# Projections of a fused block: the keys and values turned as 32-row tiles in one stretch per chunk, their sums a chunk late, the queries' relu moved from GpSimd to VectorE

## What is computed

```python
qkv = jnp.einsum('bchw,oc->bohw', gn(x), w_qkv)              # 768 channels from 256
y = depthwise 5x5 conv of qkv, then a grouped 1x1 conv
q = relu(mqkv[:, :, :DIM]); k = relu(mqkv[:, :, DIM:2 * DIM]) # mqkv: qkv and y, by heads
v = jnp.pad(mqkv[:, :, 2 * DIM:], one row of ones)
vk = jnp.einsum('bhdn,bhen->bhde', v, k)                      # sums over all points
out = jnp.einsum('bhde,bhen->bhdn', vk, q)
out = out[:, :, :-1] / (out[:, :, -1:] + ATT_EPS)             # then w_proj and a scale and shift
x = x + out
```

## Time and profile before

| | |
|---|---|
| median of 3 runs | 2473.91 us (2470.03 to 2474.42) |
| the profiled execution, its span | 2473.8 us |
| PE busy | 2359.6 us, 95% |
| VectorE busy | 1994.9 us, 81% |
| ScalarE busy | 1495.6 us, 60% |
| GpSimd busy | 1099.8 us, 44% |
| the page's slices 5 to 17, the projections | PE 9 (99 for most), DVE 7 or 8, ACT 5 or 6, POOL 7 or 8 tenths |
| products of the projections (L1132), 2304 matmuls | 319.2 + 303.5 + 301.9 us |
| GpSimd's relu of the queries (L939), 126 instructions | 239.1 us |

### The profile page before, as it was taken

The page is one execution under the profiler, slowest core; times in us unless marked ns, Lnnn a source line. Parts: engine busy times, 40 slices in busy tenths (PEclk is TensorE's granted clock), DMA queues, the critical chain, the costliest instruction groups (busy, mean ns, idle before and its releaser), DMA issues. The chain is left out here.

```text
span 2473.8 us, 66794 instructions
## 1 busy us (share of the span) xinstructions
PE 2359.6 (95%) x25485; PEld 1881.3 (76%) x25485; DVE 1994.9 (81%) x2653; ACT 1495.6 (60%) x1864; POOL 1099.8 (44%) x1476
## 2 busy tenths in 40 slices
PE   5999799999999999799999999999999889999998
PEld 5889688877777887577888888888888656666666
DVE  7887688878788877778888888888888588888775
ACT  5777566666566666566776776677767434433442
POOL 7722387887787878200000000000000068888887
PEclk9999899999999999899999999999999999999999
DMA  7874689988988989988888888888888777777774
GB/s 285 336 301 173 208 295 344 329 293 314 316 288 323 344 299 302 253 196 207 209 209 208 209 210 207 210 208 209 207 208 210 228 243 280 275 275 271 271 272 136
DMA packets 300973, 628.38 MB, mean 254 GB/s; under 512 B 50784, under 2 KB 252256, under 8 KB 291552
## 3 DMA queue, kind: packets, MB, share of 16 engines
q1 hardware_dynamic: 295072, 590.38, 77.5%
q10 hardware_dynamic: 4688, 31.63, 3.6%
q0 software_dynamic: 1008, 3.67, 0.4%
HBM read 327.81 MB, written 300.94 MB: 254 GB/s over the span
## 5 line engine op out<-in xcount | busy, mean ns | idle before, releaser
L1562 PE MATMUL c_ps<-dh,wh 128*128 128x512 f32 x1152 | 465.3, 404 | 15.8 <-DVE wl L1712 9.9
L1477 ACT ACTIVATE dh<-image 128x1632 fp32r<-128x1632 f32 x192 | 301.5, 1570 | 269.9 <-PE c_ps L1562 254.8
L1562 PE MATMUL c_ps<-dh,wl 128*128 128x512 f32 x1152 | 456.4, 396 | 0.0
L1562 PE MATMUL c_ps<-dl,wh 128*128 128x512 f32 x1152 | 454.6, 395 | 1.6 <-issue 1.6
L1921 POOL TENSOR_TENSOR ql<-image,qh 128x1024 fp32r<-128x1024 f32 x1 | 2.4, 2359 | 967.8 <-DVE ql L2152 967.8
L1670 DVE TENSOR_TENSOR dl<-image,dh 128x1632 fp32r<-128x1632 f32 x192 | 356.3, 1856 | 73.9 <-ACT dh L1477 73.9
L1132 PE MATMUL o_ps<-xh,wqh 128*128 128x512 f32 x768 | 319.2, 416 | 11.3 <-issue 8.4
L1909 POOL TENSOR_TENSOR ql<-image,qh 128x1024 fp32r<-128x1024 f32 x126 | 300.9, 2413 | 10.7 <-ACT qh L1940 10.7
L1132 PE MATMUL o_ps<-xl,wqh 128*128 128x512 f32 x768 | 303.5, 395 | 0.0
L1132 PE MATMUL o_ps<-xh,wql 128*128 128x512 f32 x768 | 301.9, 393 | 0.0
L1562 PEld LDWEIGHTS c_ps<-dh,wh 128*128 128x128 f32 x1152 | 218.5, 190 | 68.6 <-DVE wl L1712 10.0
(11 more groups left out here) (212 smaller groups left out, 5107.8 us busy)
## 6 DMA issues: line engine op xcount, KB each, us to landing
qkv_scratch<-stage SPq DMA_DIRECT2D x384, 408.0 KB, 4.7
image<-qkv_scratch SPq DMA_DIRECT2D x189, 816.0 KB, 6.3
yq_scratch<-qy SPq DMA_DIRECT2D x64, 512.0 KB, 6.7
image<-qr_scratch SPq DMA_DIRECT2D x128, 256.0 KB, 6.1
image<-yq_scratch SPq DMA_DIRECT2D x128, 256.0 KB, 5.3
ox<-x_scratch SPq DMA_DIRECT2D x8, 4096.0 KB, 15.3
qr_scratch<-qs SPq DMA_DIRECT2D x126, 256.0 KB, 3.6
out<-ox SPq DMA_DIRECT2D x7, 4096.0 KB, 12.7
```

The source lines that it names most:

```text
L1477: act.activation(dh[kind][:, :], raw[kind], ACT.Copy).then_inc(hi_ready, 1)
L1562: last = pe.matmul(c_ps[:, m, :], w[hp][:, kind, part, o:o + P], cells[:, :, HALF * dy:HALF * dy + HALF * NB], start=(k == 0), stop=(k == 5))
```

## The change

In `projections`:

- The turns become 64 transposes of 32 rows by 128 columns (`turn(n)`), all in one stretch after product 5, into four banks (`t_ps` has one for each 32 rows; keys in the left half, values in the right). ScalarE reads them in two instructions of 128x1024, `take_k` and `take_v`, at the start of the next chunk.
- The sums of chunk n - 1 stand after product 5 of chunk n, in front of the turns; those of the last chunk come after the loop.
- The waits for the sums and turns (`small_ready`) are set in front of the last matmul of product 5. They have a new one: in chunk 5 it waits for `var`, since `stat_ps` is now the first four columns of a turned bank; in chunk 1 for the reading of the sums. The matmul of the means waits for ScalarE's readings of the chunk before.
- VectorE reads the sums in chunk 1 of the next image, after the queries' differences. The mean is copied out of PSUM first. `variance()` stands before the copy of product 5.
- The queries' relu `qs` goes from GpSimd (two instructions of 128x512) to VectorE (one of 128x1024), behind the queries' differences.
- `pause` goes. GpSimd's `edge` is now a tensor_tensor with a column of zeros as one operand. The border's memset stands between edge and copy.

In `output`, the table `K["vk"]` has B + 1 places, and its two halves are read by instructions of their own.

```diff
@@ projections, GpSimd
-                        pause(1 + u, n)
+                        if u == 0 and n % 4 < 2:
+                            queries_free(pool, b, n)
                         edge(kv, 2 * u, 2 * u, n)
+                        if u == 0 and n % 4 < 2:
+                            border(n)
                         pool.tensor_copy(staged(2 * u, n, 2), every_second(kv, 2 * u, n, 1 - n % 2)).then_inc(kv_odd, 1)
...
                         if n % 2:
-                            pool.tensor_scalar(staged(j0, n, 0, 0, 1), every_second(buf, t0, n, 0, 1), -1.0, None, ALU.mult)
+                            pool.tensor_tensor(staged(j0, n, 0, 0, 1), none, every_second(buf, t0, n, 0, 1), ALU.subtract)
                         else:
-                            pool.tensor_copy(staged(j0, n, 1, HALF - 1, HALF), every_second(buf, t0, n, NB - 1, 1))
+                            pool.tensor_tensor(staged(j0, n, 1, HALF - 1, HALF), every_second(buf, t0, n, NB - 1, 1), none, ALU.add)
...
-                        for t in range(2):
-                            last = pool.tensor_scalar(qs[:, n % 2, t, :], qw[:, n % 2, t, :], 0.0, None, ALU.max)
-                        last.then_inc(qs_ready, 1)
@@ projections, ScalarE
+            def take_k(g):
+                act.wait_ge(t_full, 2 * g + 2)
+                at_least(act, vk_full, g)
+                act.activation(kT[:, :, :, :].rearrange("p u a (r c) -> p r (u a) c", r=NSQ),
+                               kt_ps.rearrange("p r (a c) -> p r a c", c=SQ), ACT.Relu).then_inc(k_turned, 1)
...
+                        if before:
+                            take_k(g - 1)
                         key(0)
+                        if before:
+                            take_v(g - 1)
@@ projections, TensorE
                     for w, xx in ((wh, xh), (wl, xh), (wh, xl)):
+                        if k == 5 and ahead is not None:
+                            ahead()
...
+            def small_ready(b, n):
+
+                g = NCH * b + n
+                at_least(pe, k_turned, g)
+                at_least(pe, v_turned, g)
+                if n == 1:
+                    at_least(pe, vk_taken, 2 * b)
+                if n == 5 and not (isinstance(b, int) and b == B - 1):
+                    pe.wait_ge(ns["var"], b + 2)
...
+                pe.wait_ge(kv_ready, 2 * g + 2)
+                pe.wait_ge(kv_ready_v, 2 * g + 2)
+
+            def turn(n):
+
+                for s, out in ((0, kt_ps), (1, vt_ps)):
+                    for u in range(2):
+                        for a in range(4):
+                            for r in range(NSQ):
+                                rows = slice(SQ * r, SQ * r + SQ)
+                                last = pe.transpose(out[:, r, SQ * (4 * u + a):SQ * (4 * u + a) + SQ],
+                                                    kv[rows, n % 2, 2 * u + s, P * a:P * a + P], K["ident"][rows, rows])
+                    last.then_inc(t_full, 1)
...
                         product(b, n, 2)
-                        turn(b, n, 0)
...
                         product(b, n, 3)
-                        product(b, n, 4)
                         if variances:
                             variances()
-                        turn(b, n, 1)
-                        product(b, n, 5)
-                        for u in range(2):
-                            sum_vk(b, n, u)
+                        product(b, n, 4)
+                        product(b, n, 5, lambda: small_ready(b, n))
+                        if not (isinstance(b, int) and b == 0 and n == 0):
+                            sum_vk((n - 1) % NCH)
+                        turn(n)
@@ projections, VectorE
+                        at_least(dve, K["qr_stored"][n % 2], 32 * (4 * b + n // 2))
+                        dve.tensor_scalar(qs[:, n % 2, :, :], qw[:, n % 2, :, :], 0.0, None, ALU.max).then_inc(qs_ready, 1)
...
                         if n > 0:
                             queries(n - 1)
+                        if n == 1 and not (isinstance(b, int) and b == 0):
+                            sums_out(b - 1, bass.ds(B if isinstance(b, int) and b == 1 else b - 1, 1))
...
+                        if nxt and n == 5:
+                            variance()
                         dve.wait_ge(o_full, QT * g + 6)
@@ output, VectorE
-                for c in range(2):
-                    last = dve.tensor_tensor(ks[par][:, :, c, HT * c:HT * c + HT], heads.unsqueeze(1).broadcast_to([P, KT, HT]),
-                                             at[:, :, 0, D:D + 1].broadcast_to([P, KT, HT]), ALU.mult)
+                for t, at in halves:
+                    for c in range(2):
+                        last = dve.tensor_tensor(ks[par][:, t:t + 2, c, HT * c:HT * c + HT], heads.unsqueeze(1).broadcast_to([P, 2, HT]),
+                                                 at[:, :, 0, D:D + 1].broadcast_to([P, 2, HT]), ALU.mult)
```

## The result

| | before | after |
|---|---|---|
| median, 4 runs each | 2474.16 us | **2616.57 us** (2614.77 to 2619.55) |
| ratio, 95% interval | | **1.0576** [1.0563, 1.0589] |
| span of the profiled execution | 2473.8 us | 2617.8 us |
| TensorE's start in the next stage | 1005.3 us | 1151.3 us (+146.0) |

The rest of the program is 2 us shorter, so all of the loss lies in the projections. The direction was forecast, the size was not: +57 against +142.

The account below looks back on a forecast made before the run. TensorE bounds the projections; after the change VectorE's chain, with 0.5 us slack, would set most chunks. Ordinary 19.5, chunk 1 8.2, chunk 0 -4.8, chunk 5 30.8 + 0.5, ends and output 3: +57, 2531 us, range 2464 to 2564.

Parts of the forecast that it names:

- What bounds the kernel: Projections: TensorE is the bound, busy 88.6 of 89 us an image; VectorE's real slack is 0.5 us a chunk.
- TensorE's part: Each chunk: two stretches of turns out, one of 64 small turns in, -0.6 us; TensorE would allow a 10.3 us period.
- Ordinary chunks: 39 chunks (2, 3, 4, 6, 7 of eight images, without the last): VectorE sets the period, +0.5 us each, +19.5.
- GpSimd's reads: VectorE's chain: GpSimd's SBUF reads hold two-input instructions; 1.2 us a chunk in place of 0.97, so +0.23.
- Rival B: VectorE's chain: relu and `xl` both held by a GpSimd copy, 1.65 us a chunk; 2548 us in all, chance 0.18.
- The clock: Chunk 5 only: after some 4 us idle TensorE's granted clock falls to 0.50, adding 1.1 us.
- The stream: The 64 turns take 1.12 us as in the convolution stage; their going one after another was given nothing.
- Chunk 1: Eight chunks at +0.5 us, plus 0.6 in seven for reading the sums before the second value copy: +8.2.
- Chunk 5: Seven images: TensorE's last matmul of product 5 waits for `var` behind `xl`, +4.4 us each, +30.8.
- The signs: Expected after: TensorE waiting 0.5 to 1 us for `xl`, busy below 85 of 90, turns 1.1, chain 8.1 or more.
- Rival A: GpSimd's reads fall under copies from PSUM, the 0.97 us of collisions goes to zero: 2462 us, chance 0.15.
- The port pair: By the skill's whole-instruction lock, GpSimd's reads would cost VectorE 3.4 us a chunk, over 100 in all.

Follow-up runs that it names:

- e: Kernel before with the queries' relu on VectorE, waiting additions out and two-input edges; turns, sums and statistics as before: 2524.41 us, 1.0206.
- q: g with the turns as 16 transposes of 128x128 in place of 64 of 32 rows: 2464.97 us, 0.9955.
- m: h with the turns as 16 transposes of 128x128 in place of 64 of 32 rows: 2463.75 us, 0.9952.
- r: m with the turns as 32 transposes of 64 rows in place of 16 of 128x128: 2446.69 us, 0.9889.
- h: g with product 0 starting with its four matmuls of `xh` and waiting for `xl` only behind them: 2495.52 us, 1.0102.
- f: Kernel after with three more matmuls of 128x512, never read, behind each chunk's turns: 2592.66 us, 1.0471.
- g: c with `variance()` moved up behind the second value copy of chunk 5: 2497.05 us, 1.0093.
- d: Kernel after with `variance()` moved up in chunk 5, in front of the differences of keys and values 1: 2576.97 us, 1.0409.
- c: Kernel after with the relu on GpSimd again and GpSimd's waiting additions and one-input edges back: 2519.82 us, 1.0174.
- b: Kernel after with GpSimd's waiting additions and one-input edges back; the relu stays on VectorE: 2544.82 us, 1.0276.
- s: e with 48 never-read matmuls of the sums' form (96 instructions) between each chunk's sums of u = 0 and 1: 2691.80 us, 1.0878.
- o: e with 48 small never-read transposes added behind each chunk's sums: 2780.61 us, 1.1239.

## Why the prediction was wrong in size, step by step

**What bounds the kernel, TensorE's part.** Right. The slack of VectorE was as read: e, which lengthens its chain alone, is 51 us slower. q, m and r show the other side of it: with VectorE's chain left alone and few enough instructions, TensorE's savings come through. The turns take 1.1 us, a chunk of h 10.2 (forecast 10.3).

**Ordinary chunks: the step that failed.** Forecast +19.5 for the 39 of them, measured +88.9 (443.3 to 532.3 us). Of these e, with the same work on VectorE and the clock full, has 39.8, twice the forecast; the other 49 are slow clock, for the most part, and stalls, which the sum put at nothing in these chunks. Three terms:
- GpSimd's reads. I had counted 1.65 us a chunk and then took 1.2, because the relu, with one input, was "mostly not" held. It is: 1.07 against 0.72. The row that I relied on the earlier trace rows was of an instruction half as long in another stage. The full count gives 3.03 + 7.21 + 0.65 + 0.68 + 0.14 = 11.71, and the trace shows 11.8. Rival B's mechanism held, not its 2548, which leaves out clock and stalls as well (and by its own 0.45 for each of the 54 chunks would have been 2555). The relu's own 0.75 was right (0.72).
- The clock. I charged it only behind the 4 us idle of chunk 5. It also falls behind two idles of 0.5 and 0.8 us with the sums and turns between them, and costs about 1.5 us in each of 28 of the 39 chunks, some 42 us. No row of before had shown a fall without a long idle, and I took that for a condition; f shows that filling the idle brings the clock back in about half of these chunks.
- The stream. Forecast nothing ("the rows of the convolution stage are the same instruction"). The time of an instruction was right, but not that so many could be had. The stage from which I took the row has as many small ones beside 54 long matmuls in 14.5 us, 12.5 instructions a us; a chunk of 10.2 us with 36 long ones asks for 16. The stalls in the turns and at the loop's turn are 25 us in the stage, where before it was 4.5, and each is followed by slow matmuls; q to g puts 32 us on the 64 turns as such.

**Chunk 1**: +8.2 forecast, +18.5 measured, three of the eight with a stall. **Chunk 0**: -4.8 and -0.9. **Chunk 5**: +30.8 forecast for seven, **+34.7 measured**; after to d and c to g give 40 and 23 for the wait. That the sum came so near is in part luck, as its pieces did not. The order was as read, `var` directly behind `xl` and the products behind it; in image 6:

```profile
1008.40 1.65 DVE L1248 TENSOR_TENSOR xl<-xn,xh 128x1024 fp32r<-128x1024 f32 x1
1009.97 0.15 DVE L134 TENSOR_SCALAR p_ve<-pt_ps 128x2 f32<-128x2 f32 x1
```

```profile
1010.33 0.47 PE L1133 MATMUL o_ps<-xl,wqh 128*128 128x512 f32 x1 [2.59 <-issue]
1010.74 0.77 PE L1168 MATMUL psum_ps<-vT,kT 128*32 128x33 f32 x64
1011.43 1.87 PE L1159 MATMUL pt_ps<-ident,kv 32*128 32x32 f32 x64
```

TensorE starts 0.2 us after `var`, and the turns then take 1.87 us at the lower clock. But the idle is 2.4 to 2.6 us in place of 4. I had VectorE work on end from one `xl` to the next, 12.9 us; here it takes 14.6 (995.45 to 1010.05), because it waits 2 us for product 1, in front of which stand an idle of TensorE of 0.96 us without a semaphore and seven matmuls at the lower clock:

```profile
1001.12 0.69 DVE L1302 COPY kv<-o_ps 128x512 f32<-128x512 f32 x1 [1.99 <-PE o_ps L1133]
```

So my sum had too much idle in front of the last matmul, and nothing for a slow start of the chunk.

**Ends**: 3 forecast; 146.0 less the 142 of the chunks leaves 4. **Transfers**: nothing, as said; in image 6 they fell from 0.90 to 0.73 busy.

**The signs.** Most of those I named came: TensorE busy 94.2 of 109.7, held for `xl` by up to 1.2 us, the 64 turns in 1.1, VectorE's chain over 8.1, the low clock behind the hold in chunk 5. Two were off: that hold was 2.4 to 2.6 us and not some 4, and the relu was not "near 0.75" in the full change. Rival A fell: GpSimd's reads did not get out of the way.

**The port pair.** The Trainium skill ("SBUF — State Buffer", section "Who interferes with whom") has the port pair as a lock, which VectorE's 2-port modes take as well, and so this relu. On the relu the trace agrees: 1.07 against 0.72. The price that I had drawn from it, the whole copy each time, is too high: after against b, relu and `xl` take 0.35 us more in the mean, less than the 0.64 that a copy of GpSimd takes alone. How much of a copy was still to run when VectorE asked, the rows don't show, so this is no test of the lock itself. Had I taken the rule for whether and the rows for how much, the term would have been right.

## What to carry to other kernels

When an instruction takes the slack of an engine, look at what its lateness does to TensorE's clock: here 1.3 us of idle in two pieces cost about another 1.5 in slow matmuls in 28 of 39 chunks, while one piece of 0.8 in e cost none. Count TensorE's instructions per microsecond, not only their duration; where tiles make many small ones, try the coarser tile first, as here 64 rows in place of 32, which kept the gain and lost the stalls. Measure the parts of a change alone: two that cost 7 and 25 us cost 97 together, and the part that was worth having was hidden beneath them.

## What the runs showed of the hardware

- A one-input VectorE instruction of 128x1024 takes 0.72 us in the mean with the one-element additions in front of GpSimd's pieces (b), and 1.07 without them (after), where it meets a copy of GpSimd.
- Idles of 0.5 and 0.8 us in a chunk of 11.8 with sums and turns between them are followed by 3.5 us at a granted clock of 0.51; three extra matmuls a chunk (0.7 us) leave 13 such chunks of 28 and save 24 us of the program.
- Above some 14 TensorE instructions a us (an estimate from h and s) the engine stalls for 1 to 6 us without a semaphore. Each of 99 such stalls ends 2.2 to 2.9 us after an instruction packet of 16 KB starts.
- 48 transposes that all use one row tile and write one place take 66 ns each (o); over four row tiles of 32 they take 17 ns each (after), over two of 64 rows 35 ns (r).
